# Cross attention and a 32-expert layer: gathered rows turned by DMA from the third tile on, and a new order of VectorE's work in attention

## What is computed

```python
def attention(xn, ctx):                        # xn = layernorm(x)
    query = ctx @ Wq.T + bq                    # 1024 x 128
    key = ctx @ Wk.T + bk
    a = softmax(query @ key.T, axis=-1)        # 1024 x 1024
    return einsum('bln,bmn->blm', xn, a)
x = x + attention(layernorm(x), ctx)
h = layernorm(x)
logits = h @ gate_w.T + gate_b                 # 32 experts
topk_logits, topk_idx = top_k(logits, 4)
weight = softmax(topk_logits)
# each row goes through its 4 experts
gate = minimum(h @ w_gate[e] + b_gate[e], 7)          # 1024 -> 512
up = clip(h @ w_up[e] + b_up[e], -7, 7)
out = ((up + 1) * gate * sigmoid(1.702 * gate)) @ w_down[e] + b_down[e]
x = x + sum over the 4 experts of weight * out
```

## Time and profile before

| what | value |
|---|---|
| median of the runs | 3115.03 us |
| profiled execution | 3116.04 us |
| its span, first to last instruction | 3113.9 us |
| TensorE busy | 2948.7 us |
| VectorE busy | 1716.4 us |
| ScalarE busy | 1178.8 us |
| mean granted TensorE clock | 0.984 |

### The profile page before, as it was taken

One profiled execution on the slowest core, in us unless ns is written; L12 is line 12 of the kernel. 1 busy time (PEld: TensorE's weight loads), 2 busy tenths in 40 slices (PEclk: granted clock), 3 DMA queues, 4 the chain that ended last, 5 costly groups with the idle time before them and its releaser, 6 DMA issues.

```text
span 3113.9 us, 44999 instructions
## 1 busy us (share of the span) xinstructions
PE 2948.7 (95%) x14948; PEld 1512.9 (49%) x14949; DVE 1716.4 (55%) x2856; ACT 1178.8 (38%) x1235; POOL 563.5 (18%) x502
## 2 busy tenths in 40 slices
PE   6798988987999999999999999999999999999997
PEld 2354545553544455544445444454445444445443
DVE  3687878674454544555544555555555544553532
ACT  2332323233343433444433434444343433442422
POOL 1032322331111111111111111111111111111111
PEclk8899999988999999999999999999999999999999
DMA  6776656556554655755655756575565555565333
GB/s 192 175 182 176 176 151 174 181 159 207 158 162 101 178 140 144 220 162 159 191 141 143 224 148 195 162 227 151 151 200 155 162 157 160 155 178 139 75 66 61
DMA packets 343541, 501.38 MB, mean 161 GB/s; under 512 B 190881, under 2 KB 190881, under 8 KB 343234
## 3 DMA queue, kind: packets, MB, share of 16 engines
q0 software_dynamic: 45856, 152.33, 22.2%
q10 hardware_dynamic: 94576, 225.46, 20.4%
q1 hardware_dynamic: 203058, 122.94, 15.0%
HBM read 354.64 MB, written 112.46 MB: 150 GB/s over the span
## 4 chain that ended last, share of the span: by engine, by line
PE 75%; DVE 1%; ACT 0%; issue 0%; DMA 0%; ACTq 0%; POOL 0%; SPq 0%; POOLq 0%
PE psY L1291 24%; PE psG L1269 21%; PE psU L1269 21%; PE psX L1275 4%; PE psG L1327 3%; PE psA L1282 2%; DVE gt L1219 0%; ACT aT L1134 0%; DVE gt L1222 0%; DMA acc<-y,idxs 0%; DMA idxs<-slots 0%; ACT xT L1130 0%; ACTq L1056 0%; POOL acc L1121 0%; ACTq L1028 0%
## 5 line engine op out<-in xcount | busy, mean ns | idle before, releaser
L1291 PE MATMUL psY<-W,aT 128*128 128x512 f16 x3456 | 769.6, 379 | 23.5 <-ACT aT L1134 23.5
L1269 PE MATMUL psG<-W,xT 128*128 128x512 f16 x3072 | 686.5, 380 | 4.3 <-ACT xT L1130 4.3
L1269 PE MATMUL psU<-W,xT 128*128 128x512 f16 x3072 | 683.9, 379 | 0.0
L1291 PEld LDWEIGHTS psY<-W,aT 128*128 128x128 f16 x3456 | 336.9, 98 | 402.7 <-ACT aT L1134 27.5
L1269 PEld LDWEIGHTS psG<-W,xT 128*128 128x128 f16 x3072 | 300.5, 98 | 369.7 <-issue 9.1
L1269 PEld LDWEIGHTS psU<-W,xT 128*128 128x128 f16 x3072 | 300.6, 98 | 333.9
L1097 POOL DMA_INDIRECT acc<-y,idxs x143 | 225.3, 1575 | 1051.0 <-DVE y L1210 1008.0
L1210 DVE SCALAR_TENSOR_TENSOR y<-bias,idxs,y 128x1024 f32<-128x1024 f32 x143 | 183.7, 1285 | 389.3 <-ACT y L1141 389.3
L653 PE MATMUL psM<-W,XT 128*128 128x512 f16 x1392 | 355.9, 379 | 8.6 <-DVE xr L900 8.6
L1092 POOL DMA_INDIRECT xg<-xn_tab,idxg x145 | 156.8, 1082 | 953.1 <-PE psX L1275 902.8
L1141 ACT ACTIVATE y<-psY,idxs 128x1024 f32<-128x1024 f32 x143 | 159.2, 1114 | 438.1 <-DMA idxs<-slots 406.8
(11 more groups left out here) (157 smaller groups left out, 2634.3 us busy)
## 6 DMA issues: line engine op xcount, KB each, us to landing
stage_more<-in_L_ffn_w_down ACTq DMA_DIRECT2D x62, 1024.0 KB, 10.0
stage<-in_L_ffn_w_gate ACTq DMA_DIRECT2D x60, 1024.0 KB, 6.7
stage_more<-in_L_ffn_w_up ACTq DMA_DIRECT2D x31, 1024.0 KB, 5.6
stage<-in_L_ffn_w_up ACTq DMA_DIRECT2D x30, 1024.0 KB, 12.4
stage<-in_x SPq DMA_DIRECT2D x32, 512.0 KB, 5.4
xr<-in_x SPq DMA_DIRECT2D x32, 512.0 KB, 4.7
acc<-xr SPq DMA_DIRECT2D x32, 512.0 KB, 3.8
xn_tab<-x2h SPq DMA_DIRECT2D x32, 512.0 KB, 3.0
```

The source lines that it names most:

```text
L1269: op = pe.matmul(ps[:], xT[:, k, :, a], weights(par, c, offset + k * I, I), start=k == 0 and n == 0, stop=k == KH - 1 and n == 2)
L1291: op = pe.matmul(psY[:, h * HALF:(h + 1) * HALF], aT[:, k, :, a], weights(par, c, 2 * KH * I + k * H + h * HALF, HALF), start=k == 0 and n ...
```

## The change

In the experts, the rows in `xg` now hold the high halves first and then the low halves. In the steps of an expert's first two tiles TensorE turns the next tile's rows, now in 16 f16 transposes, and in every later step, half steps too, SyncE issues a transposing DMA from `xg` to a new tile `xT_next`, which ScalarE copies to `xT`. `evac_a` now stands before the wait for the clipped gate. In attention VectorE's layer norm is cut in `statistics` and `normalise`, with other work between; with one batch alone the low halves of a tile come one step later; small top-k operations are merged; TensorE's transposes of `xs2` stand at matmuls 16 to 23; the second batch's context and its queries and keys are done in the steps of the first batch alone; the weights' transposes share one evacuation, and the gate's follow after the first queries and keys.

```diff
-            def layernorm(which, out, src, ready, n):
+            def statistics(which, src, n):
...
+            def normalise(which, out, src, ready, n):
                 dve.wait_ge(s_rstd[which], n + 1)
...
+            def second_norm(bt, n):
+                if n >= 1 or batch(bt) > 0:
+                    alone(dve, s_x2T, tile(bt, n), s_past)
+                normalise(1, xs2[:], xr[:, n % 2, :], s_xs2, tile(bt, n))
...
                 def maximum_and_norm():
                     link(v, dve.reduce_max(mx[:, 0:1], psE[:], axis=AX_X))
                     dve.tensor_scalar(nmx[:, 0:1], mx[:, 0:1], -1.0, None, ALU.mult).then_inc(s_nmx, 1)
+                    if b2 is None and s > 0:
+                        lo_parts(s - 1)
+                    if b2 is not None and s > 0:
+                        second_norm(*late)
                     dve.wait_ge(s_x1[s % 2], per(8 * NT, b1, 16 * (s // 2 + 1)))
-                    layernorm(0, xs[:], x1[:, s % 2, :], s_xs, tile(b1, s))
+                    statistics(0, x1[:, s % 2, :], tile(b1, s))
                     dve.wait_ge(s_exp, tile(b1, s + 1))
                     link(v, dve.reciprocal(sc[:, 1:2], psm[:, 0:1]))
                     dve.tensor_scalar(sc[:, 0:1], sc[:, 1:2], S_PROB, None, ALU.mult).then_inc(s_sc, 1)
+                    normalise(0, xs[:], x1[:, s % 2, :], s_xs, tile(b1, s))
...
                 def exponent():
                     act.wait_ge(s_nmx, tile(b1, s + 1))
+                    act.wait_ge(s_alo, tile(b1, s))
...
-                held = range(10, 10 + KH)
+                held = range(16, 16 + KH)
...
             def queries_and_keys(bk):
                 pe.wait_ge(s_cTev, per(NT // 2, bk, NT // 2))
                 for n in range(4):
+                    if n == 0 and not first(bk):
+                        pe.wait_ge(s_exp, NT * batch(bk))
+                    if n == 2 and not first(bk):
+                        pe.wait_ge(s_x2, NT * (batch(bk) - 1))
+                    one_quarter(bk, n)
...
+                if b1 is not None and b2 is None:
+                    if s in CTX_ALONE:
+                        context(following(b1), s)
+                    if s in QK_ALONE:
+                        n = QK_ORDER[s - QK_ALONE[0]]
+                        one_quarter(following(b1), n)
...
-            def step(i, prev_guard):
+            def step(i, prev_guard, turn):
                 alone(sp, s_xg, 16 * i + 32, s_past)
                 load_slots(sp, idxg, i + 2, s_idxg)
+                if turn:
+                    alone(sp, s_xTev, i + 1, s_past)
+                    sp.dma_start_transpose(out=xT_next[:, :, :, :].rearrange("p a k q -> p (a k) q"), in_=xg[:, :]).then_inc(s_X, 16)
...
-                    step(t0, pair > 0 if par == 0 else None)
-                    with sp.Fori(t0 + 1, t1) as i:
-                        step(i, None)
+                    for j in range(len(CUT)):
+                        step(t0 + j, pair > 0 if par == 0 and j == 0 else None, False)
+                    with sp.Fori(t0 + len(CUT), t1) as i:
+                        step(i, None, True)
...
+            def evac_x(i, turned):
+                act.wait_ge(s_X, 16 * i + 16)
+                if turned:
+                    act.wait_ge(s_U, i)
+                src = xT_next[:].rearrange("p a k q -> p (a k q)") if turned else psX[:]
...
+                guarded(act, prev_guard, lambda: evac_a(i - 1))
                 act.wait_ge(s_gmin, i + 1)
                 act.activation(sg[:], gt[:], ACT.Sigmoid, scale=ALPHA).then_inc(s_sig, 1)
-                guarded(act, prev_guard, lambda: evac_a(i - 1))
...
             def transpose_rows():
-                for n in range(KH):
-                    op = pe.transpose(psX[:, n * P:(n + 1) * P], xg_w[:, n * P:(n + 1) * P], ident[:])
-                op.then_inc(s_X, 1)
+                for n in range(2 * KH):
+                    op = pe.transpose(psX[:, n * P:(n + 1) * P], xg[:, n * P:(n + 1) * P], ident16[:])
+                op.then_inc(s_X, 16)
```

More of the change, by code:

```diff
@@ L315, in lagged, with quarter, quarter_order @@
             return None if first(bk) else ((bk[0], bk[1] - 1), NT + s - lag)
+        def quarter(bk, n):
+            if batch(bk) == 0:
+                return (psM_halves + psE_halves)[n]
+            return early[n] if batch(bk) == 1 else (psE_halves + psM_halves)[n]
+        def quarter_order(bk):
+            return QK_ORDER if batch(bk) == 1 else range(4)
         def par(bk):
@@ L585, in _ @@
             pe.wait_ge(s_const, 8)
[L586 to L596, removed]
+            pe.wait_ge(s_wqk, 16 * 2)
+            for n in range(2 * KC):
+                op = pe.transpose(psT[:, n * D:(n + 1) * D], wqk_in[:, n // KC, n % KC * P:(n % KC + 1) * P], ident[:])
+            op.then_inc(s_wT, 1)
+            pe.wait_ge(s_wTev, 1)
             pe.wait_ge(s_ready, 1)
@@ L622, in context, with one_quarter @@
                     alone(pe, s_ctx, per(16, bk, 16), s_past)
+                ps = first_pairs[pair] if first(bk) else psT
                 for t in range(2):
                     for c in range(KC):
-                        op = pe.transpose(psT[:, t * HALF + c * P:t * HALF + (c + 1) * P],
+                        op = pe.transpose(ps[:, t * HALF + c * P:t * HALF + (c + 1) * P],
                                           cx[:, 2 * pair + t, c * P:(c + 1) * P], ident[:])
                 op.then_inc(s_cT, 1)
+            def one_quarter(bk, n):
+                for c in range(KC):
+                    op = pe.matmul(quarter(bk, n), WT[:, n // 2, c, :], cxT[:, c, n % 2 * HALF:(n % 2 + 1) * HALF],
+                                   start=c == 0, stop=c == KC - 1)
+                op.then_inc(s_qk, 1)
             def queries_and_keys(bk):
@@ L632, in queries_and_keys, with first_energies @@
                 for n in range(4):
[L633 to L636, removed]
+                    if n == 0 and not first(bk):
[3 more added lines that the diff above has]
+                    one_quarter(bk, n)
+            def first_energies(bk):
                 pe.wait_ge(s_qkev, per(4, bk, 4))
@@ L762, in step @@
                     if s == NT - 1:
[L763 to L769, removed]
+                        pe.wait_ge(s_exp, tile(b1, NT))
+                        first_energies(following(b1))
                 if late:
@@ L902, in step @@
                     alone(dve, s_x2, tile(b2, s + 1), s_past)
-                    if late:
-                        alone(dve, s_x2T, tile(b2, s), s_past)
-                    layernorm(1, xs2[:], xr[:, s % 2, :], s_xs2, tile(b2, s))
+                    statistics(1, xr[:, s % 2, :], tile(b2, s))
+                    if b1 is None or s == NT - 1 or own is False:
+                        second_norm(b2, s)
                     if b1 is None and s >= 3:
@@ L1294, in down, with step @@
                 op.then_inc(s_Y, 1)
-            def step(i, e, par, first, prev_guard):
+            def step(i, e, par, first, prev_guard, turned):
                 def weights_cut(chunks):
```

174 lines of the change are left out of this document (92 added, 82 removed).

## The result

The changed kernel takes 3225.07 us in the median of four runs (3223.42 to 3233.96), against 3115.53 us before: a ratio of 1.0356, 95% interval 1.0336 to 1.0376. The forecast was 2980 us with a range of 2952 to 3022, so it was wrong, and in sign. The changed kernel's profiled span is 3222.4 us.

What follows compares the result with a forecast made beforehand. TensorE, busy 95% of the span, was taken to bound the kernel, with VectorE's chain setting attention's steady steps. 3116.0 less 90.6 (experts) and 44.1 (attention) gave 2981.3, 2980 us against the median; range 2952 to 3022.

Steps and rivals of the forecast that it cites:

- Turns off TensorE, -70.4 us: Expert stage: the transposing DMA takes over 80 of 145 turned tiles, each 0.88 us of TensorE, 70.4 us saved.
- f16 turns: Expert stage: the 65 turns left on TensorE become 16 f16 transposes, 0.93 us each, +3.3 us together.
- aT first, -23.5 us: Expert stage: ScalarE copies psA before waiting for the clipped gate, so 17 waits for aT, 23.5 us, go.
- I take 0 us exposed: Expert stage: transposing DMAs land and are copied before the next gate product, costing 0 us; 32 x 1 us kept for range.
- The deadline: Expert's fourth tile, the tightest case: 13.4 us left for the transposing DMA to land, after allowing 1.2 us for the copy.
- Rival 3: Expert stage: transposing DMAs beside weight loads land in 19.6 us, 6.2 late in 32 experts, 198 us; 3178 us; chance 4%.
- Attention, -44.1 us: All of attention: steady steps, first batch alone, hand-over, later boundaries and start together save 44.1 us.
- The start: Attention's start: context pairs in separate banks and context issued three small loads earlier, 5 us saved.
- The first batch alone: Attention steps with one batch, all VectorE in series: 8.52 us steps fall to 7.7, 6 us saved.
- The hand-over: Attention, from batch 0's last maximum to batch 1's first: 22.4 us becomes 14.9, 7.5 saved.
- the two boundaries: Attention's later batch boundaries: queries no longer wait for xr, 2 waits, 6.4 us saved.
- the steady steps: Attention with both batches under way: 17.50 us steps become 16.3, or 17.2 when turning context, TensorE setting them; 19.2 us saved.

Runs made afterwards that it cites:

- e1: The changed kernel, but TensorE turns the rows of every tile and no transposing DMA is left in the experts: 3030.42 us, ratio 0.9727.
- e8: As e2, transposing DMAs only from an expert's fourth step on (48), but TensorE's second and third steps share one loop body: 2991.5 us, ratio 0.9599.
- e3: The changed kernel with later experts' weight loads cut to 64 columns of 128 rows each, for its time alone: 2958.11 us, one run.
- e4: The kernel before with one edit, ScalarE copies psA ahead of its wait for the clipped gate: 3091.96 us, ratio 0.9925.
- e6: e1 with attention's second layer norm normalised right behind its statistics again, ahead of the next maximum: 3043.88 us.
- e2: The changed kernel with transposing DMAs only from an expert's fourth step on (48), TensorE's third step written out once more: 3101.03 us, ratio 0.9953.

## Why the prediction was wrong, step by step

- **Turns off TensorE, -70.4 us: right.** e1 less e8 is 38.9 us for 48 turns, 0.81 each; e3 is 72.3 us below e1.
- **f16 turns: right.** 16 transposes took 0.90 us (1325.46 to 1326.36, the psX and psY starts of a step) where I had 0.93. The Trainium skill ("TensorE: Matmul & The Clock Gate", back-to-back issue gap) has a sustained 81 ns a matmul of 128 columns, which makes an estimate of 1.30 us; the trace has 56 ns, and this measurement decides.
- **aT first, -23.5 us: right,** and shown alone by e4.
- **"I take 0 us exposed": this failed,** and it carries the sign. The deadline was right for full tiles: 13.4 us from issue. The landing was not: I took 4.3 to 9.8 us from attention. The 9.8 there ran beside a load of 2 MB and one of 0.5 MB that stood ahead on their own queue, the others beside no weight loads. In an expert's third step 3 MB of weights on ScalarE's queue start within a microsecond of it and 1 MB of bias in the next 4 us. The 30 landings are 17.9 to 21.6 us. With 19.3 as their middle, 5.9 us are over the deadline; measured are 199.8 us of new waits over 30, 6.7 each. For the 21 full tiles it is 6.1 us each. For the nine half tiles it is 8.0: there TensorE does psA first, which needs ScalarE's copy of xT and then `ahl`, and the prediction had no deadline for them. I had the loads in that very step in my text and still gave them 1 us for the range. The rows to read were the second tile's loads themselves: in the stretch of the earlier trace rows they are issued at 1302.0 to 1305.3, just when I let the transposing DMA start at 1302.7, the two of w_down land in 9.9 us in the middle and the last bias in 12.9, at 1318.2, 15.5 us after that start.

```profile
stage_more<-in_L_ffn_w_down ACTq DMA_DIRECT2D x2, 1024.0 KB, 9.9
...
bias<-in_L_ffn_b_down ACTq DMA_DIRECT2D x1, 512.0 KB, 12.9
```

- **Rival 3** named the mechanism, the place and nearly the price (6.2 us by 32, 198 us), but with a chance of 4%. What spoke against it, that twice 9.8 us is nowhere in the trace, was no evidence: the trace had no transposing DMA beside weight loads. Its 19.6 us was twice the longest seen and came from no row; that it lies near the 19.3 is luck.
- **A cost in no rival: the clock, 64.2 us.** Each of the 30 idle stretches, 5.0 to 9.1 us long, is followed by matmuls at the low clock, 0.63 us instead of 0.38, for 2 to 6 us. Even with rival 3 certain, the sum would have been 3178 us; with the clock it is 3242, and 3220 with attention's better result; measured 3225.
- **Attention, -44.1 us: right in sign, a third too small; 66.2 measured.** The start gave 8.9 (first maximum at 37.36 instead of 46.26; I had 5). The first batch alone gave 11.1 (48.4 us for seven steps instead of 59.5; I had 6). The hand-over gave 6.3 (7.5), the two boundaries 6.4 (6.4). Most of the miss is in the steady steps, which gave 33.9 where I had 19.2: the 21 from xr to xr within a batch took 366.2 us before and 332.3 now. They repeat every 15.84 us where I had 16.3 and 17.2. My slip: I let a product start when xr is ready, but TensorE first does energies and rank, so xr's latency and part of xs's are already past; the xs wait is 9.8 us over 14 times, not 1.0 in each. VectorE's 15.9 us, which I had computed and put aside, is what sets the step; e6 shows it.

Two VectorE steps of the changed kernel, the xr instructions of the earlier trace rows, which e6's 16.56 us stand against:

```profile
299.47 1.22 DVE L938 SCALAR_TENSOR_TENSOR xr<-psM,xr 128x1024 f32<-128x1024 f32 x1
...
315.31 1.22 DVE L938 SCALAR_TENSOR_TENSOR xr<-psM,xr 128x1024 f32<-128x1024 f32 x1
```

What stays open: why the loads themselves take as long as they do beside the scatter and the transposing DMA. The equal numbers of packets say in what order the queues are served, not how long each turn takes.

## What to carry to other kernels

A transfer moved onto the DMA queues has the landing time of the step where it will run, beside what runs there, and not that of the same instruction elsewhere. Look at what each queue issues in the microseconds around it, at how long those transfers last, and at who has the more packets: here a transfer of 2224 small ones could not end before one of 1503 large ones. If it must share a step with large loads, issue the loads after it has landed: here that turned 3.6% slower into 4.5% faster. Where a late operand makes TensorE idle for several microseconds, add the matmuls that follow at the low clock, here a third of the waits again.

## What the runs showed of the hardware that was not expected

- A transposing DMA of 0.5 MB lands in 4.2 to 4.4 us alone, and in 17.9 to 21.6 us when 3 MB of loads on another queue start with it, though its own packets use the 16 engines for some 3 us in both. While it meets them, the queues send equal numbers of packets whatever their size (66, 67 and 67 of three queues in 2 us). SyncE's queue is held for up to 17.43 us by issuing one.
- Writing one step out again in TensorE's program (e2) brought 128 more packets in the instruction queue and 15 waits of up to 12.1 us, 110 us in all (3101.0 less 2991.5) with the matmuls at the low clock behind them; the same work in a loop (e8) had none of it.
- 16 f16 transposes of 128 x 128 take TensorE as long as 8 f32 ones: 0.90 against 0.88 us.
